# A state-space layer and a wide FFN on one core: state products in row halves, the step by transposes, and a new split of the diagonal terms between VectorE and GpSimd

## The reference

```
n = layernorm(x)
x_inner, z = split(n @ in_proj_w.T)                      # 512 channels each
x_conv = silu(causal_conv4(x_inner) + conv_b)
dt, B, C = split(x_conv @ x_proj_w.T)                    # 1, 16, 16 per token
delta = softplus(dt);  A = -exp(A_log)                   # 16 states per channel
h_t = h_(t-1) * exp(delta_t A) + x_t * delta_t B_t;  y_t = h_t . C_t
x = x + ((y + x_conv * D) * silu(z)) @ out_proj_w.T
h = butterfly_up(layernorm(x) @ W_exp + b_exp)           # 1024 hidden
x = x + butterfly_down(gelu(h + up_bias)) @ W_con + b_con + down_bias
```

## Time and profile before

| | |
|---|---|
| median of 3 runs | 567.76 us (567.37 to 569.14) |
| the profiled execution | 569.59 us, of which the span of the profile is 567.9 |
| PE busy | 528.9 us (93% of the span), DVE 409.6 (72%), ACT 306.1 (54%), POOL 109.5 (19%) |
| mean granted TensorE clock | 0.966 of full speed |
| phases 2 to 6 | 61.6 us each |

### The profile page before, as it was taken

How to read it: one execution, slowest core, us unless ns; L and a number is a source line. 1 busy time by engine, 2 the same in 40 slices (tenths; PEclk the granted TensorE clock), 3 DMA queues, 4 the chain that set the end, 5 groups by cost and what they waited for, 6 DMA issues and landing times.

```text
span 567.9 us, 8152 instructions
## 1 busy us (share of the span) xinstructions
PE 528.9 (93%) x2996; PEld 430.3 (76%) x2996; DVE 409.6 (72%) x860; ACT 306.1 (54%) x526; POOL 109.5 (19%) x96
## 2 busy tenths in 40 slices
PE   3998899888999999999999999999999999699896
PEld 3766676776897779887888778877888788578886
DVE  4859999587983799468966799379946894575532
ACT  2876883865239622874268623962287417431342
POOL 4042100230201301050103120130105021411110
PEclk9986979799999999999999999999999999799999
DMA  8542311200012001210112001200021002100011
GB/s 244 97 27 3 80 35 38 76 2 2 23 52 74 4 2 48 66 39 2 37 41 74 0 9 68 71 8 1 5 73 38 0 2 74 41 1 0 6 34 37
DMA packets 42619, 21.75 MB, mean 38 GB/s; under 512 B 26419, under 2 KB 41011, under 8 KB 42580
## 3 DMA queue, kind: packets, MB, share of 16 engines
q1 hardware_dynamic: 39940, 17.57, 13.0%
q10 hardware_dynamic: 2640, 3.67, 2.3%
...
...
## 4 chain that ended last, share of the span: by engine, by line
PE 48%; DVE 20%; issue 12%; ACT 9%; SPq 6%; POOL 3%; DMA 0%; DVEq 0%; ACTq 0%; POOLq 0%
PE wide L711 12%; PE acc L844 9%; PE wide L833 7%; SPq L420 5%; PE wide L822 4%; DVE xc L1552 2%; DVE xc L1555 2%; POOL x1b_xn L598 2%; DVE state L1516 2%; DVE hid_low L1429 2%; PE wide L804 2%; PE small L731 2%; PE wide L811 2%; DVE xc L1412 2%; ACT L1054 2%
## 5 line engine op out<-in xcount | busy, mean ns | idle before, releaser
L1054 ACT ACTIVATE hid_f<-wide,bias_up 128x512 f32<-128x512 f32 x64 | 44.0, 687 | 162.0 <-PE wide L833 161.6
L1412 DVE SCALAR_TENSOR_TENSOR xc<-xi,taps,xc 128x512 f32<-128x512 f32 x96 | 87.0, 911 | 4.0 <-ACT xc L1085 1.7
L844 PE MATMUL acc<-w_down_high,hid_high 128*128 128x256 f32 x256 | 73.2, 286 | 5.6 <-DVE hid_low L1429 5.4
L844 PE MATMUL acc<-w_down_high,hid_low 128*128 128x256 f32 x256 | 71.9, 281 | 0.0
L844 PE MATMUL acc<-w_down_low,hid_high 128*128 128x256 f32 x256 | 71.9, 281 | 0.0
L1429 DVE TENSOR_TENSOR hid_low<-hid_f,hid_high 128x512 fp32r<-128x512 f32 x64 | 46.3, 725 | 29.8 <-ACT hid_high L1163 29.2
L833 PE MATMUL wide<-xnT_ln2T_high,w_up_high 128*128 128x512 f32 x128 | 55.4, 432 | 3.4 <-DVE xnT_ln2T_low L1423 1.8
L522 POOL TENSOR_TENSOR rstd<-var_eps,minus_half 128x4 f32<-128x4 f32 x16 | 19.1, 1192 | 202.8 <-DVE var_eps L1317 202.8
L711 PE MATMUL wide<-xnT_ln1T_high,w_in_high 128*128 128x512 f32 x128 | 56.5, 441 | 1.1 <-DVE xnT_ln1T_low L1423 1.0
L822 PE MATMUL wide<-w_out,xc 128*128 128x256 f32 x256 | 56.7, 379 | 0.3 <-DVE xc L1555 0.3
L844 PEld LDWEIGHTS acc<-w_down_high,hid_high 128*128 128x128 f32 x256 | 48.0, 188 | 11.2 <-issue 8.2
...
## 6 DMA issues: line engine op xcount, KB each, us to landing
...
```

The lines of the kernel that those rows point to most:

```text
L844: last = pe.matmul(acc[:, c, :], hid[h][:, j % HRING, c * P:(c + 1) * P], w_down[w][:, j, 0:DM], start=j == 0 and c % 2 == 0 and n == 0, s ...
L1054: ins = act.activation(out_ap, in_ap, how.pop("func"), **how)
L1412: ins = dve.scalar_tensor_tensor(xc[u % BATCH][:, e, :], xi[:, e, tap:tap + TILE], taps[:, e, tap:tap + 1], xc[u % BATCH][:, e, :], ALU.mu ...
```

## The change

1. `ssm_output_halves` replaces `ssm_output` from unit 1 on. A `y` bank now holds two channel blocks for half the tokens. The products with `m_mat` are the same in number and size. The state products go over 64 rows of `state` and 256 columns, alternating between rows 0-63 (first bank) and rows 64-127 (second bank). The second pair of blocks comes after `up` 3 and `down` 1. On DVE `gates_of_halves` adds in quarters of 256 columns and then multiplies by z.
2. The step, B and C numbers go back to token order by transposes; DVE's copy becomes a sum over the two halves.
3. Gaps times rates moves from POOL to DVE, right after the scan. POOL multiplies `c_near` by B in place (`b_with_c`) between `mask_b` and `place_c_block`, and DVE multiplies `diag` by that. POOL adds bias and residual at the head of the next unit's work, not after its gates.
4. On DVE `advance_state` comes before `assemble`, and the convolution of block 1 moves ahead of the second `low_hidden`. ACT loads the gelu table before it waits for `up` 0.
5. In phase 7 `up` 0 to 2 come before `step_sums`, and ACT and DVE split `ln2T` before the exp table and the softplus.
6. The last `down` products, the last addition and the last store go in two halves of the tokens. At the start POOL makes the masks before the permutations.

The core of the diff:

```diff
-            def diagonal_times_b(u):
-                wait(pool, diag_exp, u, 1)
-                pool.tensor_tensor(diag[:, :, :, :], diag[:, :, :, :],
-                                   dB[:, :, :].unsqueeze(2).to_broadcast([P, GR, BL, NS]), ALU.mult)\
-                    .then_inc(diag_times_b.handle, 1)
+            def b_with_c(u):
+                wait(pool, dB_ready, u, 1)
+                wait(pool, c_spread, u, 16)
+                near = c_near[:, :, :, :]
+                pool.tensor_tensor(near, near, dB[:, :, :].unsqueeze(1).to_broadcast([P, BL, GR, NS]), ALU.mult)\
+                    .then_inc(b_times_c.handle, 1)
...
             for u in range(UNITS):
+                if u:
+                    residual_with_bias(u - 1)
                 weigh_gaps(u)
                 mask_b(u)
-                diagonal_gaps(u)
+                b_with_c(u)
                 place_c_block(u)
-                diagonal_times_b(u)
                 if u + 2 < UNITS:
                     rstd_of(u + 2, 0, var1, rstd1)
-                if u:
-                    wait(pool, gated, u, CB)
-                    residual_with_bias(u - 1)
                 rstd_of(u, 1, var2, rstd2)
...
                 for c in range(GR):
-                    last = pe.matmul(bank[:, c * P:c * P + XD], xdT[:, c * P:(c + 1) * P], fold[:, :], start=True, stop=True)
+                    last = pe.transpose(bank[:, c * P:(c + 1) * P], xdT[:, c * P:(c + 1) * P], ident[:, :])
                 mark_written(last, "xdtok", 0, u)
...
+            def ssm_output_halves(u, pair):
+                banks = [tile_of("y", 2 * pair + h, u) for h in range(2)]
+                for h in range(2):
+                    free(pe, u, "y", 2 * pair + h)
+                if pair == 0:
+                    read(pe, u, "moff", 0)
+                for q in range(2):
+                    g = 2 * pair + q
+                    for c in range(GR):
+                        at = q * HALF_TILE + c % 2 * P
+                        pe.matmul(banks[c // 2][:, at:at + P], x_tok[:, c, g * P:(g + 1) * P],
+                                  m_mat[:, c * P:(c + 1) * P], start=q == 0 and c % 2 == 0, stop=False,
+                                  skip_group_check=True)
+                if pair == 0:
+                    read(pe, u, "ct", 0)
+                    wait(pe, first_state, u, 1)
+                    wait(pe, states_ready, u, 1)
+                for q in range(2):
+                    g = 2 * pair + q
+                    for h in range(2):
+                        rows = slice(2 * SLOT * h, 2 * SLOT * (h + 1))
+                        last = pe.matmul(banks[h][:, q * HALF_TILE:(q + 1) * HALF_TILE],
+                                         state[u % BATCH][rows, g * P:(g + 1) * P],
+                                         c_startT[rows, h * HALF_TILE:(h + 1) * HALF_TILE],
+                                         start=False, stop=q == 1, skip_group_check=True)
+                        if q == 1:
+                            mark_written(last, "y", 2 * pair + h, u)
...
                 in_or_none(v, 3)
+                if v == UNITS:
+                    for j in range(3):
+                        up(p, j)
                 step_sums(u)
...
                 beside("products")
-                up(p, 0)
-                up(p, 1)
-                beside("up 1")
-                up(p, 2)
+                if v < UNITS:
+                    up(p, 0)
+                    up(p, 1)
+                    beside("up 1")
+                    up(p, 2)
                 down(p, 0)
-                ssm_output(u)
+                ssm_output_halves(u, 0)
                 up(p, 3)
                 down(p, 1)
+                ssm_output_halves(u, 1)
                 up(p, 4)
...
                 transposes(u, "ln2T", xn2, norm2)
-                for j in range(HB + 2):
-                    if j < HB:
-                        up(u, j)
+                for j in range(HB):
+                    up(u, j)
                     if j >= 2:
                         down(u, j - 2)
+                first, second = range(GR // 2), range(GR // 2, GR)
+                down(u, HB - 2, first)
+                down(u, HB - 1, first).then_inc(first_half_down, 1)
+                down(u, HB - 2, second)
+                down(u, HB - 1, second)
...
                     take_x_tok(u, c)
+                if v == UNITS:
+                    high_parts(p, "ln2T")
                 load_exp_table()
...
                 copy_first_state(u)
+                load_gelu_table()
                 gelu(p, 0)
...
                 written(dve, u, "xdtok", 0)
-                mark_read(dve.tensor_copy(xd[:, :, :], tile_of("xdtok", 0, u)[:, :]
-                                          .rearrange("p (c w) -> p c w", w=P)[:, :, 0:XD]), "xdtok", 0, u)
+                mark_read(dve.tensor_reduce(xd[:, :, :], tile_of("xdtok", 0, u)[:, :]
+                                            .rearrange("p (c h w) -> p c w h", h=2, w=HALF)[:, :, 0:XD, :], AXIS_X, ALU.add), "xdtok", 0, u)
                 read(dve, u, "xdtok", 0)
...
                 read(dve, u, "sums", 0)
-                wait(dve, diag_gaps, u, 1, ago=1)
-                dve.tensor_tensor_scan(gaps[:, :, :].rearrange(flat), restart[:, :, :].rearrange(flat),
-                                       d_block[:, :, :].rearrange(flat), 0.0, ALU.mult, ALU.add)\
-                    .then_inc(gaps_ready.handle, 1)
+                link(dve.tensor_tensor_scan(gaps[:, :, :].rearrange(flat), restart[:, :, :].rearrange(flat),
+                                            d_block[:, :, :].rearrange(flat), 0.0, ALU.mult, ALU.add))
+                dve.tensor_tensor(diag[:, :, :, :], gaps[:, :, :].unsqueeze(3).to_broadcast([P, GR, BL, NS]),
+                                  rates[:, :].unsqueeze(1).unsqueeze(1).to_broadcast([P, GR, BL, NS]), ALU.mult)\
+                    .then_inc(diag_gaps.handle, 1)
...
-                wait(dve, diag_times_b, u, 1)
-                wait(dve, c_spread, u, 16)
+                wait(dve, diag_exp, u, 1)
+                wait(dve, b_times_c, u, 1)
                 link(dve.tensor_tensor(diag[:, :, :, :], diag[:, :, :, :], c_near[:, :, :, :].rearrange("p u c n -> p c u n"),
...
+            def gates_of_halves(u, pair):
+                own = xc[u % BATCH]
+                if pair == 0:
+                    wait(dve, z_ready, u, 1)
+                for h in range(2):
+                    written(dve, u, "y", 2 * pair + h)
+                    tokens = slice(h * HALF_TILE, (h + 1) * HALF_TILE)
+                    for q in range(2):
+                        g = 2 * pair + q
+                        ins = dve.scalar_tensor_tensor(own[:, g, tokens], own[:, g, tokens], skip[:, g:g + 1],
+                                                       tile_of("y", 2 * pair + h, u)[:, q * HALF_TILE:(q + 1) * HALF_TILE],
+                                                       ALU.mult, ALU.add)
+                        if q:
+                            mark_read(ins, "y", 2 * pair + h, u)
+                        else:
+                            ins.then_inc(skipped.handle, 1)
+                wait(dve, skipped, u - 1, 2 * pair + 2)
+                for h in range(2):
+                    read(dve, u, "y", 2 * pair + h)
+                for g in (2 * pair, 2 * pair + 1):
+                    dve.tensor_tensor(own[:, g, :], own[:, g, :], z[u % BATCH][:, g, :], ALU.mult).then_inc(gated.handle, 1)
...
                 take_xd(u)
+                if v == UNITS:
+                    low_parts(p, "ln2T")
                 softplus(u)
-                low_parts(p, "ln2T")
+                if v < UNITS:
+                    low_parts(p, "ln2T")
                 beside("softplus")
...
                 sum_diagonal(u)
+                advance_state(u)
                 assemble(u)
...
                 low_hidden(p, 0)
-                advance_state(u)
+                if v < UNITS:
+                    convolve(v, 1)
                 low_hidden(p, 1)
...
                     first_stats(r)
-                gate(u, 0)
-                gate(u, 1)
+                gates_of_halves(u, 0)
                 low_hidden(p, 2)
...
                     first_normalise(r)
-                gate(u, 2)
-                gate(u, 3)
-                if v < UNITS:
-                    convolve(v, 1)
+                gates_of_halves(u, 1)
                 low_hidden(p, 3)
...
             low_hidden(UNITS - 1, *range(HB))
-            final(UNITS - 1)
+            last, h = UNITS - 1, GR // 2
+            wait(dve, x1b_ready, last, 1)
+            dve.wait_ge(first_half_down, 1)
+            dve.tensor_tensor(x1b[:, 0:h, :], acc[:, 0:h, :], x1b[:, 0:h, :], ALU.add).then_inc(first_half_final, 1)
+            written(dve, last, "down", 0)
+            mark_read(dve.tensor_tensor(x1b[:, h:GR, :], acc[:, h:GR, :], x1b[:, h:GR, :], ALU.add), "down", 0, last)
```

61 lines of the change are left out of this document (31 added, 30 removed).

## The result

The changed kernel takes **584.1 us** (median of 4 runs, 583.48 to 584.96) against 567.57 of the kernel before in the same comparison: ratio 1.029, 95% interval 1.026 to 1.032. The forecast was 575.0 (562 to 583): slower, as said, but by 16.5 us instead of 7.2. In the profiled executions the span grows by 15.4 us, from 567.9 to 583.2.

| part | before | after | change | forecast |
|---|---|---|---|---|
| phase 0, from the span's start | 96.85 | 105.95 | +9.1 | +9 |
| phase 1 | 75.29 | 81.25 | +6.0 | +1 |
| phases 2 to 5, mean of one | 61.69 | 60.83 | -0.9 | -1.0 |
| phase 6 | 59.77 | 60.54 | +0.8 | -1.0 |
| phase 7 up to `out_projection` | 39.97 | 43.91 | +3.9 | +3 |

A forecast was written before the change was run, and what follows sets the result against it. PE, busy 528.9 of 567.9 us, was taken to bound the kernel. Phase terms 9 + 1 - 5 + 3 and the end's -0.8 made +7.2 us on 567.76: 575.0 us, range 562 to 583.

The forecast's parts named there:

- Phase 0, +9: POOL's B-times-C product, waiting for C, delays cbd_tok; PE waits 8.4 us more, then half clock; +9 us, bounds +6 and +11.
- Phase 1, +1: POOL's product within DVE's weight additions and state steps before low down weights, against 1.8 us of output: +1, bounds -1, +3.
- Phases 2 to 6, -1 each: In each of five phases, down 0 comes 0.8 us later and the output gains 1.8 us: -1.0 each, -5 together.
- The wait before `down` 0: In phase 4, PE idles 1.5 us ahead of down 0, which starts 0.8 us later than before.
- the pairs: State products on different 64-row halves run two at once, 1.65 us instead of 3.3 a phase, plus 0.15 per shape change.
- the vanished bank wait: PE's 0.42 us wait for a bank in the output goes, since up 3 and down 1 lie between.
- POOL's hold: DVE's c_start stands still during POOL's 2.38 us product of B and C, coming at 373.65 instead of 370.5.
- Phase 7, +3: down 0 comes 2.2 us late, low clock costs 2 to 3, output returns 1.4: +3 us, bounds -4 and +6.
- The end, -0.8: Halving the last 1.23 us addition and sending half the store ahead gives -0.8 us, bounds 0 and -1.2.
- A: Rival: POOL and DVE run beside each other, c_start is ready early, phases 1 to 6 gain 2.3 each; 561 us, chance 0.17.
- B: Rival: unit 0's wait is taken up and the clock stays up, +9 becomes +2; 568 us, chance 0.12.
- C: Rival: the row halves run one after the other, losing 1.65 us in seven phases; 586.5 us, chance 0.07.

The follow-up runs named there:

- the exchange in unit 0 alone: Changed kernel, but in unit 0 alone POOL runs place_c_block ahead of b_with_c; 576.3 us, ratio 1.014.
- the exchange in every unit: Changed kernel with POOL's place_c_block ahead of b_with_c in all units: 568.5 us, ratio 1.001; with further edits also 561.0, 567.6 and 558.4 us.
- the cut product: Changed kernel with POOL's product of B and C cut from 1024 to 64 elements a partition from unit 1 on; 578.9 us, ratio 1.018.

## Why the prediction was right in sign and wrong in size

- **Phase 0, +9:** measured +9.1. The mechanism, POOL's order, is as named, and the exchange in unit 0 alone takes most of it back. That the size fits is partly luck. The wait was 9.7 us and not 8.4, the output came 11.3 us late, and 2.3 came back because it ran at full clock, where the prediction had it at half clock again. Other traces of kernels with this order have phases 0 of 104.0 to 108.4 us.
- **Phase 1, +1: this is the step that failed.** Measured +6.0. Two causes of its order part were named (the product in the weight additions, the state steps before the low down weights), but they were set off against 1.8 us of a faster output and priced too low: the waits there are 1.46, 1.32 and 1.86 us longer, and the output, from its first product to `out_projection`, gave 0.9 (13.57 to 12.64). A third cause, POOL's addition beside DVE's normalisation, was not seen. Order makes somewhat over 3 us. The rest is clock, which the sum charged in phases 0 and 7 only. What decides how much half clock falls into phase 1 stays open: the kernels with the exchange in every unit have nearly the same waits there (2.8, 2.1, 1.6 and 1.5 us among them) and 0, 6.8 and 13.7 us of half clock.
- **Phases 2 to 6, -1 each:** -0.9 in four. The wait before `down` 0 (1.47), the pairs (1.06) and the vanished bank wait are as forecast. The terms are a little off against each other: `down` 0 comes 1.2 us later in three of the four (0.7 in unit 5's, forecast 0.8), the output gave 1.6 (14.23 to 12.65, forecast 1.8), and 0.3 behind `out_projection` stood in no sum. Phase 6 gave +0.8: it had no bank wait before to lose, so its output gave only 0.5 (12.69 to 12.17), with 0.24 of waiting for DVE's last gate in it, while `down` 0 is 1.2 later there too. Counting it as a fifth cost 1.8 us of error. POOL's hold, as the cut product showed, makes 0.65 us of the lateness and nothing of the wait of 1.47, which is DVE's state steps.
- **Phase 7, +3:** +3.9, with the wait before `down` 0 (6.06 us) where it was put; but `step_sums` was late for PE's `up` products, which themselves waited 2.56 us and then ran at low clock, and not for DVE. The output was to give 1.4; at full clock, in the run with the old order of phase 7, it gives 0.5.
- **The end, -0.8:** -1.0.
- **Rivals.** A is out (DVE stands still beside POOL's product, 2.41 us for 64 elements), B is out (phase 0 grew by 9.1 us), C is out (1.06 against 1.92). The measured 584.1 lies beyond the range's end of 583, and the bound of +3 for phase 1 is one that was crossed.

The Trainium skill (SBUF — State Buffer, Who interferes with whom) lists, beside DVE instructions with two SBUF inputs, `tensor_scalar` in its two-port mode as one that shares the port pair with GpSimd. The trace agrees: DVE's normalisation, one tensor input, took 3.41 us for four where it takes 1.38, beside POOL's addition. In which mode it ran, no trace here shows. The prediction looked for holds only at products of two tensors and so left this one out, 2 us of DVE's time. What PE lost by it shows in phase 1 of the run with the row halves alone and of the one with the addition moved, both at full clock: the next wait for ACT, whose exp comes behind this step of DVE, grows from 1.03 to 1.58 us.
